# Four elementwise steps of the bidirectional recurrence moved from VectorE to GpSimd in a two-layer attention and feed-forward kernel

## What is computed

```python
ek = jnp.exp(jnp.minimum(kf, 30.0)); ekv = ek * vf
def step(carry, x):
    a, b = carry; ekv_t, ek_t = x
    a = a * decay + ekv_t
    b = b * decay + ek_t
    ...
_, (nf, df) = lax.scan(step, init, (ekv_t, ek_t))
_, (nb, db) = lax.scan(step, init, (ekv_t, ek_t), reverse=True)
euk = jnp.exp(jnp.minimum(u + kf, 30.0))
num = nf + nb - ekv + euk * vf
den = df + db - ek + euk
base = jax.nn.sigmoid(r) * (num / jnp.maximum(den, 1e-08))
out = base * (0.8 + 0.2 * tf)
```

## Time and profile before

| | |
|---|---|
| times of the runs | 832.2, 836.22, 967.87 us, median 836.22 |
| span of the profiled execution | 830.0 us (the runs nearest to it lie 2.2 and 6.2 us above) |
| busy PE / DVE / ACT / POOL | 509.5 / 553.3 / 299.9 / 226.2 us |
| end of the first layer | the quantisation maximum at 310.4 us |
| busy to 311 us, DVE / POOL | 255.6 / 10.1 us |

### The profile page before, as it was taken

One profiled execution on the slowest core, in us unless ns is written; L12 is line 12 of the kernel. 1 busy time (PEld: TensorE's weight loads), 2 busy tenths in 40 slices (PEclk: granted clock), 3 DMA queues, 4 the chain that ended last, 5 costly groups with the idle time before them and its releaser, 6 DMA issues. The chain is left out here.

```text
span 830.0 us, 17909 instructions
## 1 busy us (share of the span) xinstructions
PE 509.5 (61%) x7444; PEld 422.6 (51%) x7444; DVE 553.3 (67%) x1066; ACT 299.9 (36%) x716; POOL 226.2 (27%) x320
## 2 busy tenths in 40 slices
PE   0363557865958533455556565757777660899980
PEld 0253446754747423334444453545555450899980
DVE  6999699897689847757617772556664155667834
ACT  3363423642556220064440522443313150365520
POOL 3000000000000001007817818803850026043344
PEclk9775666977889776755588576868979655899996
DMA  8435050050000103740250032200101062656214
GB/s 310 160 65 105 1 115 1 2 114 1 2 1 1 51 0 70 152 88 4 54 102 7 8 71 53 48 6 7 11 9 12 11 276 81 255 192 224 95 54 136
DMA packets 52066, 61.29 MB, mean 74 GB/s; under 512 B 25408, under 2 KB 45392, under 8 KB 47504
## 3 DMA queue, kind: packets, MB, share of 16 engines
q1 hardware_dynamic: 50176, 55.15, 24.9%
q0 software_dynamic: 1808, 4.99, 2.0%
HBM read 45.24 MB, written 13.63 MB: 71 GB/s over the span
## 5 line engine op out<-in xcount | busy, mean ns | idle before, releaser
L881 PE MATMUL psum<-arena 32*32 32x16 f32 (+16 forms) x5608 | 354.0, 273 | 232.3 <-DVE arena L1550 74.5
L881 PEld LDWEIGHTS psum<-arena 128*32 128x32 f32 (+7 forms) x5608 | 282.7, 128 | 302.6 <-DVE arena L1550 76.8
L1987 POOL TENSOR_TENSOR arena<-arena 128x31 f32<-128x31 f32 (+15 forms) x124 | 68.0, 548 | 9.7
L1985 POOL TENSOR_TENSOR arena<-arena 128x31 f32<-128x31 f32 (+15 forms) x124 | 64.4, 519 | 9.7
L1343 ACT ACTIVATE psum<-psum,arena 128x256 f32<-128x256 f32 (+7 forms) x128 | 45.7, 370 | 26.8 <-DVE arena L1611 26.6
L1312 ACT ACTIVATE arena<-psum 128x512 f32<-128x512 f32 (+1 forms) x48 | 35.3, 736 | 48.3 <-PE psum L881 48.2
L1621 DVE TENSOR_REDUCE arena<-psum 128x2 f32<-128x512 f32 (+1 forms) x48 | 41.3, 860 | 13.6 <-PE psum L881 12.9
L1520 DVE TENSOR_TENSOR_SCAN arena<-arena 128x255 f32<-128x255 f32 x64 | 42.5, 726 | 11.4 <-ACT arena L1255 11.3
L1965 POOL DMA_DIRECT2D arena<-wq x1 | 0.9, 862 | 171.9 <-PE psum L881 171.9
L1998 POOL TENSOR_TENSOR fc_second_parts<-arena,fc_first_parts 128x2048 fp32r<-128x2048 f32 x6 | 27.9, 4648 | 63.8 <-ACT fc_first_parts L1431 63.8
L1255 ACT ACTIVATE arena<-arena 128x255 f32<-128x255 f32 x64 | 27.2, 498 | 46.6 <-DVE arena L1506 46.6
(11 more groups left out here) (179 smaller groups left out, 955.6 us busy)
## 6 DMA issues: line engine op xcount, KB each, us to landing
arena<-fc SPq DMA_DIRECT2D x16, 1024.0 KB, 5.2
arena<-parts SPq DMA_DIRECT2D x40, 256.0 KB, 4.6
parts<-arena SPq DMA_DIRECT2D x16, 384.0 KB, 3.5
arena<-parts SPq DMA_DIRECT2D x40, 128.0 KB, 5.5
dispatched<-arena SPq DMA_DIRECT2D x1, 2048.0 KB, 18.5
arena<-arena SPq DMA_DIRECT2D x128, 8.0 KB, 1.8
arena<-dispatched SPq DMA_DIRECT2D x8, 256.0 KB, 3.0
expert_rows<-arena SPq DMA_DIRECT2D x8, 256.0 KB, 2.3
```

The costliest lines, as they stand in the source:

```text
L881: return nc.tensor.matmul(out, lhsT, rhs, start=start, stop=stop)
L1985: link(G_.tensor_tensor(tmp, A3[:, k + 1:BLK, k:k + 1].to_broadcast([P, rows, w]), X3[:, k:k + 1, 0:w].to_broadcast([P, rows, w]), ALU.mult))
L1987: ins = G_.tensor_tensor(X3[:, k + 1:BLK, 0:w], X3[:, k + 1:BLK, 0:w], tmp, ALU.add)
```

## The change

`weigh` is split. VectorE keeps L1529, L1532, L1533 and the reciprocal, which now counts a new semaphore `den_ready`. GpSimd gets a `weigh` part of five instructions: two that need only `euk` (minimum and time factor, then times the value), and after `den_ready` three more (numerator, swapped quotient, gate product). The time factor goes into `ekv` in step `values`, so that the numerator carries it. `wkv` n now waits on VectorE for `gate_ready` of n-2, and `gate` waits for its own `gate_ready`. `gate(0,0)` moves behind `wkv(0,1)` and its `scale`; `gate(0,1)` moves behind `keys(2)`, `keys(3)` and `values(2)`. A third buffer `eukvs` is added.

```diff
-    both(("keys", 0), ("values", 0), ("wkv", 0, 0), ("scale", 0, 0), ("keys", 1), ("back", 0, 0), ("weigh", 0, 0), ("gate", 0, 0))
-    both(("values", 1), ("wkv", 0, 1), ("scale", 0, 1), ("back", 0, 1))
+    both(("keys", 0), ("values", 0), ("wkv", 0, 0), ("scale", 0, 0), ("keys", 1), ("back", 0, 0), ("weigh", 0, 0))
+    both(("values", 1), ("wkv", 0, 1), ("scale", 0, 1), ("gate", 0, 0), ("back", 0, 1))
...
-    both(("largest", 0), ("split", 0, 0), ("weigh", 0, 1), ("gate", 0, 1), ("keys", 2), ("keys", 3), ("values", 2))
+    both(("largest", 0), ("split", 0, 0), ("weigh", 0, 1), ("keys", 2), ("keys", 3), ("values", 2), ("gate", 0, 1))
...
-                    link(V.tensor_tensor(ekv[:, :, bt(b)], ek[:, :, bt(b)], fsT[:, :, bt(b)], ALU.mult))
+                    link(V.scalar_tensor_tensor(out=ekv[:, :, bt(b)], in0=ek[:, :, bt(b)], scalar=tf[:, 3 * B + b:3 * B + b + 1],
+                                                in1=fsT[:, :, bt(b)], op0=ALU.mult, op1=ALU.mult))
...
+                    if n >= 2:
+                        dve.wait_ge(gate_ready, n - 1)
...
                     link(V.scalar_tensor_tensor(out=scan[2], in0=euk, scalar=EXP30, in1=scan[2], op0=ALU.min, op1=ALU.add))
-                    st(V.scalar_tensor_tensor(out=euk, in0=euk, scalar=EXP30, in1=fsT[:, :, bt(b)], op0=ALU.min,
-                                              op1=ALU.mult))
                     link(V.tensor_scalar_max(scan[2], scan[2], 1e-8))
                     link(V.tensor_tensor(scan[3][:, 0], scan[2][:, 0], scan[2][:, 1], ALU.mult))
-                    st(V.reciprocal(scan[3][:, 1], scan[3][:, 0]))
-                    link(V.tensor_tensor(scan[0], scan[0], euk, ALU.add))
-                    link(V.tensor_tensor(scan[1], scan[2][:, ::-1], scan[3][:, 1].unsqueeze(1).to_broadcast([P, CT, T]), ALU.mult))
...
-                    V.scalar_tensor_tensor(out=G[c % 2][:, :, bt(b)], in0=scan[0], scalar=tf[:, 3 * B + b:3 * B + b + 1],
-                                           in1=scan[1], op0=ALU.mult, op1=ALU.mult).then_inc(gate_ready, 1)
-                    dve.wait_ge(gate_ready, n + 1)
+                    V.reciprocal(scan[3][:, 1], scan[3][:, 0]).then_inc(den_ready, 1)
                 elif kind == "gate":
...
+                    dve.wait_ge(gate_ready, NUMBER["weigh", g, b] + 1)
...
+                if kind == "weigh":
...
+                    pool.wait_ge(euk_ready, CT * (n + 1))
...
+                    link(G_.tensor_scalar(eukv, euk, EXP30, tf[:, 3 * B + b:3 * B + b + 1], ALU.min, ALU.mult))
+                    link(G_.tensor_tensor(eukv, eukv, fsT[:, :, bt(b)], ALU.mult))
+                    pool.wait_ge(den_ready, n + 1)
+                    link(G_.tensor_tensor(scan[0], scan[0], eukv, ALU.add))
+                    link(G_.tensor_tensor(scan[1], scan[2][:, ::-1], scan[3][:, 1].unsqueeze(1).to_broadcast([P, CT, T]),
+                                          ALU.mult))
...
+                    G_.tensor_tensor(G[c % 2][:, :, bt(b)], scan[0], scan[1], ALU.mult).then_inc(gate_ready, 1)
+                    pool.wait_ge(gate_ready, n + 1)
```

More of the change, by code:

```diff
@@ L482, in program @@
         euks = [v3(take(CT * T), CT) for _ in range(2)]
+        eukvs = [v3(take(CT * T), CT) for _ in range(2)]
         w1 = v3(take(CT * HID), CT)
@@ L653, in program @@
         euk_ready = sem("euk_ready")
+        den_ready = sem("denominators_ready")
         scanned = sem("forward_sums_ready")
@@ L1937, in _ @@
                 kind = step[0]
-                if kind == "largest":
+                if kind == "weigh":
+                    _, c, b = step
+                    n = NUMBER[step]
+                    scan, euk, eukv = scans[n % 2], euks[n % 2], eukvs[n % 2]
+                    pool.wait_ge(euk_ready, CT * (n + 1))
+                    if n == 0:
+                        pool.wait_ge(ek_ready, 3)
+                    link(G_.tensor_scalar(eukv, euk, EXP30, tf[:, 3 * B + b:3 * B + b + 1], ALU.min, ALU.mult))
[4 more added lines that the diff above has]
+                                          ALU.mult))
+                    if c == 2:
+                        wait_pe(pool, ("proj", 0, b))
+                    elif c == 3:
+                        wait_pe(pool, ("fc1", b, 1))
+                    G_.tensor_tensor(G[c % 2][:, :, bt(b)], scan[0], scan[1], ALU.mult).then_inc(gate_ready, 1)
+                    pool.wait_ge(gate_ready, n + 1)
+                elif kind == "largest":
                     i = step[1]
```

## The result

| | before | after |
|---|---|---|
| median of the runs, us | 834.3 (4 runs, later ones included) | 875.08 (4 runs, 871.01 to 875.32) |
| ratio, 95% interval | | 1.0497 [1.0458, 1.0536] |
| span of the profiled execution, us | 830.0 | 873.1 (its own time 874.89) |
| first gate of the second layer starts, us | 314.06 | 358.01 |

The account below looks back on a forecast made before the run. It took VectorE to bound the first layer. Relief of 2.7 us in each of 16 recurrences was outweighed by waits for GpSimd and mutual exclusion: +30 us on 830.0, plus 4, gives 864 us; forecast range 853 to 878, 8-in-10 range 836 to 884.

Parts of the forecast that it names:

- the wait at the direct places: Six recurrences with `wkv` right behind `weigh`: next `wkv` 7.6 us after `weigh` starts, not 6.09, so 1.5 us later.
- the scans that GpSimd stops: VectorE scans and GpSimd instructions exclude each other, less about 0.15 us overlap; 1.6 us per early pair beside scans.
- the end: Last `weigh` to the quantisation's reduction: GpSimd done at 310.9 where the reduction started at 310.38, +0.5 us.
- early pair: GpSimd's two `weigh` instructions needing only the exponential: 2.1 us together, costing VectorE 1.6 us beside scans or splits.
- late three: GpSimd's three `weigh` instructions after the reciprocal: 1.29 us each, 4.2 us together with gaps.
- waits only: Rival: scans do not exclude GpSimd, so only waits and queue cost; +4 us, 838 us; chance 0.15.
- one-input instruction: First of GpSimd's five in `weigh`, minimum and time factor: taken at 0.7 us, upper bound the two-input price of 1.29.
- dearer: Rival: GpSimd instructions with pointer scalar, swapped half or repeated operand cost 2 us; +24 or so, 888 us; chance 0.12.
- the start: First two recurrences: `gate(0,0)` 7.3 us late through queue and exclusion, `gate(0,1)` 11.4 us late.
- the middle: Recurrences u2 to u13: direct waits and early pairs, less relief and idle waits, take the delay from 16.2 to 29.5 us.

Follow-up runs that it names:

- e1: The changed kernel with only GpSimd's order altered, largest and ternary reductions gathered behind later weighs: 859.33 us, ratio 1.0331 to the kernel before.
- e2: e1 with the last recurrence weighed wholly on VectorE again: 855.04 us, ratio 1.0297 to the kernel before.
- e6: Kernel before plus one 128x2 add on GpSimd between the last `weigh` and the quantisation's reduction: 837.62 us, ratio 1.0064.
- e7: Kernel before plus the same 128x2 GpSimd add as e6, one recurrence earlier: 832.17 us, ratio 0.9981.
- e3: e2 with a third set of scan buffers, so `wkv` waits for the `weigh` three before it, not two: 847.60 us, ratio 1.0174.
- e5: Kernel before with only `gate(0,0)` and `gate(0,1)` moved to their later places: 842.00 us, ratio 1.0131.
- e10: e1 with the last and six direct-place recurrences weighed on VectorE, `gate(0,0)` and `gate(0,1)` back right behind their weighs: 837.77 us, ratio 1.0052 to before.
- e9: Kernel before with GpSimd weighing only five recurrences that have other steps behind them, one ternary reduction moved, gates in old places: 830.32 us, ratio 0.9952.

## Why the prediction came out as it did

The time fell inside the range, 11 us above the 864. The sign was right, and so were the two costs named for it, the wait at the direct places and the scans that GpSimd stops. But the sum was short by 13.1 us of span (13.9 in the first layer), and its terms were less good than that: GpSimd's change-overs were missing from it, and others were too dear, so that the place within the range is in part luck. Delay of VectorE at the starts of `weigh` (L1529 before, L1534 after), against the sum's running total:

| at | before us | after us | measured | forecast |
|---|---|---|---|---|
| `gate(0,0)` | 22.49 | 29.54 | 7.1 | 7.3 |
| `gate(0,1)` | 42.69 | 57.09 | 14.4 | 11.4 |
| u1 | 100.86 | 126.45 | 25.6 | 13.7 |
| u2 | 119.14 | 150.48 | 31.3 | 16.2 |
| u4 | 160.57 | 193.66 | 33.1 | 19.3 |
| u5 | 171.76 | 207.72 | 36.0 | 22.4 |
| u8 | 231.34 | 264.63 | 33.3 | 23.6 |
| u10 | 255.87 | 294.86 | 39.0 | 29.8 |
| u13 | 303.31 | 340.85 | 37.5 | 29.5 |
| quantisation's reduction | 310.38 | 354.32 | 43.9 | 30 |

**The step that failed: a term was missing.** The sum lets GpSimd get to u0 right behind the reduction that ends at 74.3, and gives the end +0.5. Both treat GpSimd's queue as free once the instruction ahead has ended. In fact it stood for 6.9, 6.9, 6.6 and 6.0 us at the four change-overs. `gate(0,2)` came 26.2 us late for 14.4; 3.0 of the miss were there at `gate(0,1)`, and the change-over at u0 is the larger part of the other 8.8: the reduction ends at 89.48, L1941 starts at 96.39, the gate comes at 103.88. At the end it is nearly the whole of 43.9 - 37.5 = 6.4 against 0.5. e1 (13.9 in the first layer, with 4.4 more that it left at u2) and e2's end (6.2) put the term at some 24 us at most, since e1's order also took the early pairs of u0 and u1 out from behind the reductions; e6 shows it alone, at 5.3 us.

The rows of before could not show it. There GpSimd had hardly any elementwise work in the first layer, and the one reduction in the earlier trace rows and the one in the earlier trace rows had waited 22.95 and 35.40 us for another engine, which hides a change-over as e7 does. The Trainium skill, GPSIMD Engine Reference, section "Instruction dispatch", says that the first call to freshly loaded code on GpSimd pays about 6 us with no visible instruction in the profile. The measured gaps agree in size and in being invisible; that code is what is loaded here, no run shows. I had not weighed that section for this change, though the change alternates two kinds of work in one queue.

**Right: the direct wait.** u4: from `weigh` to the next `wkv` 201.19 - 193.66 = 7.53 us against 7.6, a wait of 4.14 against "some 4". u4, u8 and u9 each added 2.8 to 2.9 us against 3.1; u2 added 1.9 for 3.1, u10 0.4 for 1.7, and u7, as forecast, nothing. Five more waits, 1.25 us at u1, 1.07 at u3, 2.59 at u5, 0.21 at u6 and 2.57 at u11, stood where the sum had other steps cover GpSimd.

**Right in size: scans exclude GpSimd.** Beside an early pair the eight scans took 2.88 + 3.61 us where the earlier trace rows has 2.44 + 2.64: 1.4 against 1.6. Beside the late three of (0,0) four scans took 5.42 us for 2.44, and GpSimd's three 1.52 each for 1.26. The *waits only* rival, 838, falls with that, and e3 shows the same from the other side. The rule of the Trainium skill, SBUF — State Buffer, section "Who interferes with whom", which no run had shown for scans, holds for them here beside GpSimd's two-input instructions. Beside its one-input instruction, which reads SBUF as well, the trace does not agree: it took 2.42 us for the 2.01 alone and made the four scans only 0.44 longer, where a full exclusion would have cost them some 1.9 (my estimate: the 2.01 less the 0.15 of overlap).

**Mis-sized: the one-input instruction.** Taken at 0.7, bound 1.29; it took 2.0 alone and 2.42 beside scans. The *dearer* rival was right for this one instruction and wrong for the late three. (Its terms as listed, 2.1 at ten places and 0.7 ten times, add up to 28 us, not 24.) It cost little in itself, since it stands early; it did count at (0,1), u0 and u1, where the early pair itself lies on the path.

**Right: the start, until GpSimd changes over.** `gate(0,0)` came 7.1 late for 7.3; e5, where GpSimd does none of this work, has 5.5 of it, so the queue, not the exclusion, is most of it. `gate(0,1)` missed by 3.0, with a change-over ahead of its pair.

**Too dear: the middle.** From u2 to u13 the delay grew by 6.2 us where the sum had 13.3. From u6 to u7 the delay fell by 2.7 us (36.3 to 33.6) for 0.4: the early pair cost the scans 0.45 there, not 1.6, since its two-input half fell beside reductions from PSUM, and the gate waited no longer than before. From u12 to u13 it fell by 2.8 (40.4 to 37.5) for nothing, at a wait of 9.40 us for ScalarE that was 10.76 before. At u11 it grew by 1.0 where the sum let it fall by 2.0. So the forecast's 30 is near the truth for a mixed reason: a missing term of up to some 24, less about 10 that the other terms were too high. The steps taken back one by one (13.9, 3.6, 14.2, 5.6, and 8.3 from e10 to e9) make the 45.6 us from after to e9, but their sizes hold for this order only, since a delay at one place is swallowed where another already waits.

**What stays open.** Which of GpSimd's instructions share code, beyond the two kinds tried here; the 2 us that e2's profile lost in mid-layer; why the second layer's length differs by up to 9 us between profiles of kernels that are alike there.

## What to carry to other kernels

Work moved to an idle engine brings only what stands between its result and the next use: here the next `wkv` came 7.5 us behind the start of `weigh` at each of the six direct places, where it had come 6.1 behind it, and only recurrences with other steps behind them could be moved without loss (e9, at best half a per cent gained). On GpSimd count the changes between kinds of instruction as well as the instructions, and put each where the engine would wait anyway. A step pushed back to cover a slower engine has followers of its own: price what its delay starts, not the wait that it hides.

## What the runs showed of the hardware

- In these runs GpSimd stood for 5.5 to 9.0 us between a reduction across partitions and elementwise work: 5.53 (e1) to 6.18 (e2) on the way to the reduction, 6.58 (after) to 9.03 (e10) on the way from it, and 6.04 behind an add of no more than 128x2 (e6). It runs while GpSimd waits for the next instruction's data: in e7 a wait of 20 us hid it.
- GpSimd's tensor-scalar form with minimum and multiply by a pointer scalar, 128x512, took 2.0 us alone; the two-input form on as many elements took 1.26.
- VectorE's scans are stopped by GpSimd's two-input instructions for 3.0 us by three of them that take 3.8 alone (5.42 for 2.44), but hardly by the tensor-scalar form (2.88 for 2.44 beside 2.42 us of it).
